# Transposing the rows of maxima on TensorE straight to their partitions, instead of moving them there by DMA

## What is computed

```python
xn = _layernorm(x)
# A, heads (2 x 16), S = 1024
scores = einsum('bhqd,bhkd->bhqk', rope(q), rope(k)) / sqrt(8)
attn = softmax(where(causal, min, scores)); out = einsum('bhqk,bhkd->bhqd', attn, v)
# B, for c in range(6)
q = ew[c, 0] * (nodes[in_q] @ We[eq] + be[eq])      # k and v alike
o = _mha(q, k, v, Wq[c], Wk[c], Wv[c], Wo[c])       # softmax over 1024 keys, 8 heads
nodes[c] = act_w[c] * o + q
out = x + A(xn) + _layernorm(nodes[5])
```

## Time and profile before

| | |
|---|---|
| three executions | 1687.03, 1687.93, 1692.68 us (median 1687.93) |
| profiled execution, its own time | 1698.56 us |
| its span, first to last instruction | 1696.7 us |
| PE, DVE, ACT, POOL busy | 92%, 70%, 66%, 26% |
| mean granted TensorE clock | 0.95 of full speed |
| A, from 40 to 345 us; B from there | 305 us; 1352 us |

### The profile page before, as it was taken

How to read it: one execution, slowest core, us unless ns; L and a number is a source line. 1 busy time by engine, 2 the same in 40 slices (tenths; PEclk the granted TensorE clock), 3 DMA queues, 4 the chain that set the end, 5 groups by cost and what they waited for, 6 DMA issues and landing times.

```text
span 1696.7 us, 65726 instructions
## 1 busy us (share of the span) xinstructions
PE 1558.3 (92%) x25626; PEld 799.3 (47%) x25626; DVE 1187.0 (70%) x1207; ACT 1117.3 (66%) x2219; POOL 446.1 (26%) x930
## 2 busy tenths in 40 slices
PE   6999999999999899898998998989989989899995
PEld 4467676644434444344443443444434434444442
DVE  7767666687857677578676775676866857767582
ACT  3366566677857677567676775676766857676582
POOL 4321113306042151240511513315115033150110
PEclk9899999999999999999999999999999999999997
DMA  7121112233222231232222312323123222231112
GB/s 225 38 94 44 42 43 80 96 105 127 71 91 83 67 117 51 64 126 68 95 72 66 124 55 72 108 66 113 55 65 127 66 88 78 74 121 49 53 34 58
DMA packets 116109, 138.86 MB, mean 82 GB/s; under 512 B 14945, under 2 KB 90466, under 8 KB 115682
## 3 DMA queue, kind: packets, MB, share of 16 engines
q1 hardware_dynamic: 115810, 134.54, 24.9%
HBM read 65.04 MB, written 62.39 MB: 75 GB/s over the span
## 4 chain that ended last, share of the span: by engine, by line
PE 73%; DMA 12%; SPq 6%; issue 4%; DVE 2%; ACT 2%; POOL 1%; ACTq 0%; DVEq 0%; POOLq 0%
PE s L942 44%; PE cps L1033 21%; PE misc L937 9%; DMA qs<-mrows 4%; DMA dram_rec_b<-sums 3%; DMA dram_raw_b<-csb 3%; SPq L407 2%; SPq L439 2%; ACT probs L723 2%; DMA ks<-dram_qk_b 1%; SPq L480 1%; SPq L454 1%; DMA ctx_b<-dram_raw_b 0%; DMA ks<-dram_qk_a 0%; SPq L433 0%
## 5 line engine op out<-in xcount | busy, mean ns | idle before, releaser
L899 DVE TENSOR_REDUCE neg_max<-s 128x1 f32<-128x1024 f32 (+7 forms) x1024 | 1123.2, 1106 | 465.9 <-PE s L942 408.0
L723 ACT ACTIVATE probs<-s 128x512 f32<-128x512 f32 x1792 | 974.5, 598 | 438.9 <-PE s L942 432.2
L942 PE MATMUL s<-qs,ks 99*32 99x512 bf16 (+1 forms) x7680 | 689.5, 384 | 93.1 <-DMA qs<-mrows 59.6
L942 PE MATMUL s<-ks,qs 96*32 96x512 bf16 (+2 forms) x7680 | 623.3, 380 | 8.7 <-DMA ks<-dram_qk_a 4.3
L1033 PE MATMUL cps<-probs,vs 128*32 128x256 f32 (+1 forms) x7296 | 616.0, 385 | 0.3 <-ACT probs L723 0.3
L942 PEld LDWEIGHTS s<-qs,ks 99*32 99x32 bf16 x7680 | 220.2, 95 | 473.7 <-ACT probs L723 249.2
L1033 PEld LDWEIGHTS cps<-probs,vs 128*32 128x32 f32 x7296 | 250.2, 112 | 185.0 <-issue 17.7
L942 PEld LDWEIGHTS s<-ks,qs 96*32 96x32 bf16 x7680 | 225.9, 98 | 97.2 <-issue 25.2
L579 POOL TENSOR_TENSOR mparts<-neg_max,zeros 128x8 bf16<-128x8 f32 x128 | 25.7, 201 | 935.2 <-DVE neg_max L899 934.8
L942 PE MATMUL s<-mask_k,ident_h 128*32 128x128 bf16 x1024 | 101.2, 221 | 0.0
L942 PE MATMUL s<-mask_q,ident_h 128*32 128x128 bf16 x1024 | 78.6, 224 | 0.6 <-issue 0.6
(11 more groups left out here) (122 smaller groups left out, 620.2 us busy)
## 6 DMA issues: line engine op xcount, KB each, us to landing
dram_qk_b<-parts SPq DMA_DIRECT2D x48, 384.0 KB, 3.5
qs<-dram_qk_b SPq DMA_DIRECT2D x96, 192.0 KB
ks<-dram_qk_b SPq DMA_DIRECT2D x96, 192.0 KB
dram_qk_b<-parts SPq DMA_DIRECT2D x48, 256.0 KB, 3.3
dram_raw_b<-csb SPq DMA_DIRECT2D x96, 128.0 KB, 4.1
dram_qk_b<-parts SPq DMA_DIRECT2D x48, 128.0 KB, 3.4
vsrc<-srcT SPq DMA_DIRECT2D x12, 512.0 KB, 4.6
ctx_b<-dram_raw_b SPq DMA_DIRECT2D x48, 128.0 KB
```

Source lines behind the costliest of these rows:

```text
L723: nc.scalar.activation(buf[:, lo:hi], s2[bank][:, 0:hi - lo], ACT.Exp, scale=scale).then_inc(exp_done, 1)
L899: last = ve.tensor_reduce(neg_max[k % 2][:, t:t + 1], s1[n % 2][:, lo:hi], AX.X, ALU.max, negate=True)
L942: last = te.matmul(dst[c0:c0 + STRIP, :], lhsT[:, c0:c0 + STRIP], rhs, start=start, stop=stop, tile_position=(0, c0))
```

## The change

The transpose is done by eight products, one for each query tile. Each takes that tile's three columns of `mparts` as weights and writes 128 columns to partitions 96 to 98 of `misc`, so that 3 x 1024 bf16 fill the bank there. ACT copies these to rows 96 to 98 of `qs`, on the same partitions. The buffer `mrows`, its DMA and the semaphores `mrow_in` go; PE waits for ACT's copy (`mrow_sb`) instead.

```diff
-        mrows = [sb(f"mrows{s}", [3 * TB, 128], BF16) for s in range(2)]
-        misc_rows = misc[0:3 * TB, 0:64].bitcast(BF16)
+        misc_rows = misc[MROW:KALL, :].bitcast(BF16)
...
-                    if kind_at(kind, k, 1):
-
-                        sp.wait_ge(mrow_sb, u)
-                        sp.dma_start(qs[(k - 1) % RING][MROW:KALL, :].rearrange("a (i n) -> a i n", n=128),
-                                     mrows[(k - 1) % 2][:, :]).then_inc(mrow_in[(k - 1) % RING], 16)
...
                             act.wait_ge(mt_ready, u)
-                            need(act, mrow_in[(k - 3) % RING], 16 * (2 * ph + (k - 3) // RING + 1)
-                                 if kind_at(kind, k, 3) else 0)
-                            nc.scalar.copy(mrows[(k - 1) % 2][:, :], misc_rows).then_inc(mrow_sb, 1)
+                            nc.scalar.copy(qs[(k - 1) % RING][MROW:KALL, :], misc_rows).then_inc(mrow_sb, 1)
...
                             if i == 0:
-                                pe.wait_ge(mrow_in[(k - 2) % RING], 16 * (2 * ph + (k - 2) // RING + 1))
+                                pe.wait_ge(mrow_sb, u - 1)
...
-                            te.transpose(misc_rows, mparts[(k - 1) % 2][:, :], ident_h[:, :]).then_inc(mt_ready, 1)
+                            for t in range(TB):
+                                last = te.transpose(misc_rows[:, t * 128:(t + 1) * 128],
+                                                    mparts[(k - 1) % 2][:, t:3 * TB:TB], ident_h[:, :],
+                                                    tile_position=(0, MROW))
+                            last.then_inc(mt_ready, 1)
```

More of the change, by code:

```diff
@@ L300, in dual_attention_kernel @@
         qk_in = [sem(f"qk_in{n}") for n in range(RING)]
-        mrow_in = [sem(f"mrow_in{n}") for n in range(RING)]
         ctx_out = [sem(f"ctx_out{n}") for n in range(2)]
```

## The result

The changed kernel is slower: ratio to the kernel before 1.060, 95% interval 1.055 to 1.064; medians 1790.99 us (1782.36 to 1796.3, four executions) against 1688.88 us. Forecast were 1781 us and 1.055. The profiled execution took 1782.36 us, the lowest of the four, and that of the kernel before 1698.56, higher than any of its four timed ones (1687.03 to 1692.68). So the two profiles are 83.8 us apart (spans 1780.5 and 1696.7 us), the medians 102.

A forecast was written before the change was run, and what follows sets the result against it. The prediction took PE, busy 92% of the span, as the bound. Transposes 52, copy 58 + 5, less credits of 19 and 2, gave +94 us: 1792.6 us from the profiled execution, 1781 from the median, ratio 1.055; range 1708 to 1835 us.

The forecast's parts named there:

- own range: The main forecast's narrower range for the whole kernel, 1750 to 1810 us, with chance 0.72.
- Transposes: On PE, seven more transposes a unit in one column group, 0.41 us uncovered in each of 128 units: 52 us.
- rival 2: On PE, weight load and product do not overlap in a group working alone: +82 us more, 1863 us; chance 0.08.
- The copy: On ACT, 0.78 us longer ahead of the exponentials; exposed 58 us in B units and 5 in stage A.
- Step 4: In B passes, PE's rows wait goes and a 3.7 us ctx_ready stall follows: credit 19 us, plus 2 in B0.
- The DMA itself: On SyncE's queue, 128 freed issues of 0.81 us bring nothing outside the stalls named.
- Rival 1 and 4: At step 4 the stall goes, nothing follows: rival 1 1712 us, chance 0.10; 4, with cheaper units, 1646 us, chance 0.04.
- Rival 5: Whole kernel: credit and cost cancel, nothing to be measured, 1688 us; chance 0.03.
- Rival 3: On PE, the clock falls around every unit's transposes: 435 us, about 2216 us; chance 0.03.

The follow-up runs named there:

- neither: Changed kernel with one transpose instead of eight and a copy of 128 columns instead of 1024, most maxima left out; ratio 0.9875 to the kernel before, -21 us.
- four corners: Four kernels, with one or eight transposes and a copy of 128 or 1024 columns; ratios to the kernel before 0.9875, 1.0201, 1.0218 and 1.0597.
- short_copy: Changed kernel with eight transposes, but ACT copies only 128 of the 1024 columns, other maxima left out; ratio 1.0218 to the kernel before, +37 us.
- rows_first: Kernel before, with SyncE issuing the rows' DMA ahead of its wait for the reciprocals' write instead of behind the broadcast; ratio 0.994, -10 us.
- chain_early: Kernel before with the rows' DMA issued earlier, the ctx_b product in two halves, and its chain started earlier in BL and BE; ratio 0.9649, -59 us.
- four_groups: Changed kernel with its eight transposes spread over four column groups instead of one, most maxima left out; ratio 1.035 to the kernel before, +59 us.

## Why the prediction was right

The result is inside the range and the own range of the forecast, 10 us above the point. The mechanism held: eight transposes queue in one column group, the longer copy stands where PE waits for exponentials, and `ctx_ready` takes over the removed wait. How close the sum came is partly luck, for three of its sizes were off and the errors cancel. The intervals between the transposes of one step and the next show it, in us a pass, over that of the kernel before (means of the ten BL passes):

| | steps 0 to 3 | 3 to 4, with the stall | 4 to 7 | 7 to 0, with the jump | pass |
|---|---|---|---|---|---|
| neither | -0.3 | -1.5 | +0.4 | -0.8 | -2.2 |
| changed kernel | +3.1 | -3.0 | +3.5 | +2.0 | +5.6 |

The forecast had 8 x 1.01 = 8.1 us for the units, nothing for the jump and 1.7 of credit, +6.4 in all. Measured: 8 x 1.17 = 9.4 for the units and 1.1 for the jump, so the credit is 9.4 + 1.1 - 5.6 = 4.9. The 1.3 and 1.1 us that were missing from the cost stand against 3.2 missing from the credit. The credit is larger in part because the chain to the product became shorter than I had it. Timelines of DVE and POOL in the changed kernel, the pass of the wait at 494.78:

```profile
480.87 0.54 DVE L897 RECIPROCAL sums<-sums 128x64 f32<-128x64 f32 x1
...
492.31 2.34 POOL L632 TENSOR_TENSOR ctx_b<-ctx_b,rec_b 128x1024 f32<-128x1024 f32 x1 [12.67 <-DMA rec_b<-dram_rec_b]
```

From the start of the reciprocals to the end of the product this is 13.8 us; in the earlier trace rows it is 15.3, and the forecast let it become 14.6 (start 1.0 later, end 0.3 later). Term by term:

- **Transposes, 52 us forecast.** The pair is 55 ns, not 58, and load and product overlap in a group that works alone: rival 2 is out. Per B unit it is 0.38 us, which is 7 x 0.055, not 0.41. That the other groups stand meanwhile because the starts are in order was wrong (three of them start at 499.61, ahead of three transposes), but it saved nothing that the intervals show. The four corners give 58 us (short_copy less neither), of which some 10 are the longer jumps, which I had declared untouched.
- **The copy, 63 us forecast.** It takes 1004 ns against 1035; the corner gives 55 us. Per unit I had the exposure too low, 0.60 instead of 0.75, as I counted on ACT's spare time in the looser units. In exchange two of the eight units of a pass lie ahead of the wait for `ctx_b`, which grows shorter by what they are late (25.7 us in all, against 45.0 in neither); the forecast had that in the credit of step 4.
- **Step 4, 19 + 2 us of credit.** The path was right: `ctx_ready` takes over, 11 times. Both numbers of the credit were wrong. The stall is 2.3 us on average, not 3.7: the chain to the product is 1.4 us shorter than before (medians 13.5 and 14.9), where I had 0.7, and PE comes to it 0.3 us later, as two units are 1.17 each and not 1.0. And the low clock costs half of 3.4 us in seven passes of ten, 1.2 us a pass, where I had charged 2.8. That is 0.7 + 0.3 + 1.6 = 2.6 of the 3.2 us.
- **The DMA itself, nothing.** This was wrong. I had said that the freed issues bring nothing outside the stalls named; they stand ahead of the chain to `ctx_b`, which is 0.8 us shorter in neither than in rows_first, and that chain is the next stall. rows_first, which keeps the DMA and loses only the wait, gains 10 us where neither gains 21. Whether other traffic shares in the 11 us was not taken apart, nor why the chain is shorter still in the changed kernel.
- **Rival 1 and 4** needed the stall to go with nothing behind it: out. **Rival 5**, no change to be measured, is out with a ratio of 1.055 to 1.064. **Rival 3**: the steps without a stall or a jump have a clock of 1.00. Out.
- **Not foreseen:** the jump, +1.2 us of idle time in nine passes.
- **Open:** the profile pair has +84 us (A 18, B0 4, BL 56, BE 8, start and end -2), the medians +102. The rest is between executions, which spread over 14 us in the changed kernel, and no trace shows where.

## What to carry to other kernels

Before a wait is removed, look for what is ready next at the same place: here the product of `ctx_b` stood two turns behind the rows, and the wait, an estimated 8 us a pass, was worth 2 (neither) or 1 (rows_first) until the chain to that product was itself moved forward and its product halved, which with the reordered DMA was worth 5.6. A DMA that is late because of its place in a queue is cheaper to reorder than to replace. Laying data out so that a row lands on its own partition turns a copy of 24 partitions x 128 into one of 3 x 1024, four times as long, on an engine whose next result PE waits for; price a copy by its columns and by what is queued behind it.

## What was not expected of the hardware

- A loop's jump back on PE takes 3.3 to 4.6 us in some kernels (means 3.6 to 3.8) and 4.4 to 5.3 in others, whose PE instructions can be the same one by one; on ACT, VectorE and GpSimd the same jump takes 0.04 to 0.06 us. The granted clock falls behind all nine of them in the kernel before and in the changed kernel, and behind most in the others.
- Products in three column groups start ahead of products that were issued before them in the fourth: at 499.61 three scores started, and three transposes issued ahead of them from 499.66 on.
- The length of PE's idle time does not by itself tell whether the clock falls. Changed kernel: 2.64 us (494.8) left it high, 2.24 us (728.5) did not. chain_early: 1.84 us (569.0) left it high, 1.64 us (1421.0) did not. four_groups: 3.12 us (718.4) left it high. Every idle time of PE over 3.5 us in the B loops was followed by the low level.
